# A PSUM bank by name for each TensorE task, in place of three banks in strict turn

## What is computed

```
x = x + tanh(g_xattn) * attention(layernorm(x), context)
x = x + tanh(g_ffn) * ffn(layernorm(x))

attention(x, c): q = rms(x Wq'), k = rms(c Wk'), v = c Wv'     (rms over the 8 values of each head)
                 softmax(q k' / sqrt(8)) v
ffn(x):          down(silu(gate(x)) * up(x))                   gate, up: 256 -> 704, down: 704 -> 256
                 weights are integers (w - 128) * scale
```

## Time and profile before

| | us |
|---|---|
| median of 3 runs | 269.2 |
| lowest, highest | 265.5, 272.75 |
| the profiled execution | 267.05 |
| its span in the trace | 265.2 |

### The profile page before, as it was taken

How to read it: one execution, slowest core, us unless ns; L and a number is a source line. 1 busy time by engine, 2 the same in 40 slices (tenths; PEclk the granted TensorE clock), 3 DMA queues, 4 the chain that set the end, 5 groups by cost and what they waited for, 6 DMA issues and landing times.

```text
span 265.2 us, 7329 instructions
## 1 busy us (share of the span) xinstructions
PE 219.6 (83%) x2592; PEld 178.5 (67%) x2592; DVE 176.5 (67%) x583; ACT 177.8 (67%) x338; POOL 106.3 (40%) x145
## 2 busy tenths in 40 slices
PE   1663979659879999899989989998999697965864
PEld 1553758437657878688777868786878585855764
DVE  4487999934665776687658765876596674657162
ACT  3258585844867895789578867885897667534250
POOL 5012212021322463645464455446444735434451
PEclk9999597956988999999999999999999999996799
DMA  5897522233075022603160406050506070000001
GB/s 178 216 352 178 62 56 49 54 45 62 0 101 101 0 56 49 136 3 72 26 138 0 87 12 138 0 100 3 121 0 82 13 109 2 21 22 0 20 20 40
DMA packets 45127, 18.08 MB, mean 68 GB/s; under 512 B 36400, under 2 KB 44848, under 8 KB 45104
## 3 DMA queue, kind: packets, MB, share of 16 engines
q1 hardware_dynamic: 45104, 17.77, 31.6%
HBM read 7.28 MB, written 2.10 MB: 35 GB/s over the span
## 4 chain that ended last, share of the span: by engine, by line
DVE 30%; PE 29%; issue 15%; POOL 14%; ACT 7%; DMA 2%; SPq 1%; DVEq 1%; POOLq 0%; ACTq 0%
PE bank L1278 7%; PE bank L1363 5%; POOL qk_parts L422 4%; POOL qk_unit L462 4%; PE pv_ps L1242 4%; POOL h_lo L430 4%; PE bank L1388 3%; DVE sums L899 3%; DVE hidden L990 3%; PE score_ps L1223 2%; PE bank L1311 2%; DVE silu L975 2%; DMA w_raw<-L_xattn_Wv_dram 2%; POOL x_all L439 2%; PE bank L1265 2%
## 5 line engine op out<-in xcount | busy, mean ns | idle before, releaser
L526 ACT ACTIVATE probs<-score_ps 128x1024 f32<-128x1024 f32 x64 | 65.9, 1032 | 3.5 <-PE score_ps L1223 3.5
L1363 PE MATMUL bank<-x_hi,gu_hi 128*128 128x256 f32 (+1 forms) x192 | 51.0, 301 | 4.7 <-DVE hidden L990 2.0
L462 POOL TENSOR_TENSOR qk_unit<-qk_raw,root_y 128x512 f32<-128x512 f32 x16 | 17.4, 1085 | 85.4 <-DVE root_y L783 85.4
L1363 PE MATMUL bank<-x_lo,gu_hi 128*128 128x256 f32 (+1 forms) x192 | 48.4, 286 | 0.0
L1242 PE MATMUL pv_ps<-probs,v_blocks 128*32 128x128 f32 x1024 | 42.8, 286 | 6.2 <-issue 4.2
L430 POOL TENSOR_TENSOR h_lo<-hidden,h_hi 128x256 fp32r<-128x256 f32 (+1 forms) x48 | 35.3, 745 | 24.8 <-ACT h_hi L651 24.4
L1363 PEld LDWEIGHTS bank<-x_hi,gu_hi 128*128 128x128 f32 (+1 forms) x192 | 35.3, 184 | 9.5 <-DVE hidden L990 2.4
L1363 PEld LDWEIGHTS bank<-x_lo,gu_hi 128*128 128x128 f32 (+1 forms) x192 | 35.5, 185 | 0.0
L1242 PEld LDWEIGHTS pv_ps<-probs,v_blocks 128*32 128x32 f32 x1024 | 24.9, 112 | 15.5 <-issue 7.4
L640 ACT ACTIVATE tanh_g<-bank,half_gate 128x256 f32<-128x256 f32 (+1 forms) x48 | 22.8, 475 | 18.2 <-PE bank L1363 16.0
L1278 PE MATMUL bank<-w_hi,xc_hi 128*128 128x256 f32 x96 | 31.7, 330 | 2.4 <-DVE xc_lo L889 2.4
(11 more groups left out here) (108 smaller groups left out, 435.2 us busy)
## 6 DMA issues: line engine op xcount, KB each, us to landing
ctx_sb<-ctx_dram SPq DMA_DIRECT2D x16, 128.0 KB, 2.6
out_dram<-x_all SPq DMA_DIRECT2D x16, 128.0 KB, 1.8
x_all<-x_dram SPq DMA_DIRECT2D x1, 1536.0 KB, 10.5
dn_int<-L_ffn_wq_down_dram SPq DMA_DIRECT2D x1, 704.0 KB, 6.7
gu_int<-L_ffn_wq_gate_dram SPq DMA_DIRECT2D x1, 640.0 KB, 4.6
gu_int<-L_ffn_wq_up_dram SPq DMA_DIRECT2D x1, 640.0 KB, 5.7
x_all<-x_dram SPq DMA_DIRECT2D x1, 384.0 KB, 5.1
w_raw<-L_xattn_Wq_dram SPq DMA_DIRECT2D x1, 256.0 KB, 2.7
```

The lines of the kernel that those rows point to most:

```text
L462: nc.gpsimd.tensor_tensor(qk_unit[:], qk_raw[:], root_y[:, 0:2 * H].unsqueeze(2).to_broadcast([P, 2 * H, HD]), ALU.mult).then_inc(unit_rea ...
L526: nc.scalar.activation(probs[:, t % 2, :], score_ps[t % 2][:].rearrange("p h n -> p (h n)"), ACT.Exp, scale=float(HD) ** 0.5 / UNIT ** 2). ...
L1363: last = nc.tensor.matmul(bank[k][0:r, a * TOK:(a + 1) * TOK], w[:, j, a, c, 0:r], xx[:, c, :], start=(n == 1), stop=(n == (4 if wide_weig ...
```

## The change

The order of the tasks stays. Each has now a bank by name:

| bank | before, in order | after, in order |
|---|---|---|
| 0 | turn0, qk0, ffn4, out1, turn2, ffn0 | turn0, qk0, ffn4, out1, y1 |
| 1 | out0, ffn2, ffn5, v1, y0, ffn1 | v0, ffn2, ffn5, v1, turn2, ffn1 |
| 2 | v0, ffn3, turn1, qk1, y1 | out0, ffn3, turn1, qk1, y0, ffn0 |

```
-    TASKS = ["turn0", "out0", "v0", "qk0", "ffn2", "ffn3", "ffn4", "ffn5", "turn1",
-             "out1", "v1", "qk1", "turn2", "y0", "y1", "ffn0", "ffn1"]
+    BANK_OF = {"turn0": 0, "out0": 2, "v0": 1, "qk0": 0, "ffn2": 1, "ffn3": 2, "ffn4": 0, "ffn5": 1, "turn1": 2,
+               "out1": 0, "v1": 1, "qk1": 2, "turn2": 1, "y0": 2, "y1": 0, "ffn0": 2, "ffn1": 1}
+    TASKS = list(BANK_OF)
...
     def use(p, task):
 
-        pos = TASKS.index(task)
+        pos, in_bank = TASKS.index(task), BANK_OF[task]
         q = p if isinstance(p, int) else FIRST_STEADY
-        n = sum(exists(i, t) for i in range(FIRST, q + 1) for k, t in enumerate(TASKS)
-                if k % NBANK == pos % NBANK and (i < q or k <= pos))
-        each = len(TASKS[pos % NBANK::NBANK])
-        return pos % NBANK, n if isinstance(p, int) else n + each * (p - FIRST_STEADY)
+        n = sum(exists(i, other) for i in range(FIRST, q + 1) for k, other in enumerate(TASKS)
+                if BANK_OF[other] == in_bank and (i < q or k <= pos))
+        each = list(BANK_OF.values()).count(in_bank)
+        return in_bank, n if isinstance(p, int) else n + each * (p - FIRST_STEADY)
```

## The result

| | before | after |
|---|---|---|
| median us | 268.73 (265.5 to 272.75, 4 runs) | 259.12 (257.91 to 259.8, 4 runs) |
| profiled execution us | 267.05 | 259.8 |
| its span us | 265.2 | 256.9 |

The changed kernel is faster: the ratio is 0.968, with a 95% interval of 0.958 to 0.977. Medians in this document are of all executions, ratios of those that took at most 1.5% more than the fastest of their kernel, so a ratio can differ a little from the quotient of two medians. Lines of the changed kernel stand 3 higher than those of before: L1265 is L1268, L990 is L993 and so on.

The account below looks back on a forecast made before the run. TensorE, busy 83% of the span, was taken as the bound. Steady rounds 3.8 us plus tail 3.2 less 0.1 in round 0 gave 6.9 us off the 269.2 us median: 262.3 us, range 257.5 to 268.5.

Parts of the forecast that it names:

- The bound and the wait: Mid-run: TensorE is the bound; turn0 idles 1.17 us a round for its bank alone, behind VectorE's late `hidden`.
- Steady rounds: Rounds 3 to 6, turn0 to qk0: 0.95 us gained a round, 3.8 us in four (2.0 to 4.7).
- At qk0: Round 5: qk0 follows v0 by 0.71 us and, 0.05 after `xc_lo`, starts at 161.02, 0.04 late.
- Shorter waits: Tasks with less cover, thinnest y0 behind qk1's copy (0.12 us less 0.05 delay): cost 0, bound 0 to 0.1 a round.
- C: Rival, y0 in rounds 2 to 6: qk1's copy slips, y0 loses 1.6 us a round, 270.4 us; chance 0.08.
- Round 0: Preparation under ffn0's name waits for y0's subtraction instead of turn2's: -0.1 us, bounded by 0 and 0.63.
- Tail: Rounds 7 to 9: 1.89 us kept through round 8 plus 1.29 in round 9, 3.2 us gained (1.5 to 4.5).
- The last group: Round 9, y0 and y1: only four products remain behind GpSimd's last `h_lo`; 1.29 us gained (0.7 to 1.51).
- the clock: Round 8: shorter gaps might keep the granted clock up, some 2.8 us more; left out of the sum, put in the range.
- D: Rival, whole round: the wait only moves, VectorE's chain closes the round; no gain, 269.2 us; chance 0.10.
- B: Rival at qk0: late `xc_lo` halves the gain to 0.5 us a steady round, 265.7 us; chance 0.22.

Follow-up runs that it names:

- this part alone: Changed kernel with the new banks kept in rounds -1 to 6 and the old strict turn in rounds 7 to 9: 263.02 us against 267.33, ratio 0.984.
- late-copy kernel: Changed kernel with ScalarE's copy of qk1, which frees y0's bank, put behind the next exponential: 263.37 us against 267.49, ratio 0.982.
- exchanged kernel: Changed kernel with the banks of turn0 and out0 exchanged in every round: 265.69 us against 267.33, ratio 0.991.
- the better table: Changed kernel with other banks for turn2, y0, y1, ffn0 and ffn1 in round 8 alone: 254.45 us against 269.01, ratio 0.950.
- either order tried on VectorE: Kernel before, old banks, VectorE's three qk_double copies moved behind both `hidden` (260.93 us, ratio 0.971) or behind the next round's `xc_lo` (262.75 us, ratio 0.978).

## Why the prediction came out as it did

The forecast was 262.3 us from 269.2, a ratio of 0.974; measured were 259.12 us and 0.968. The mechanism was right, and 6.9 us was short of the gain by terms that the sum did not hold.

**The bound and the wait.** Right. TensorE is the bound, and the idle at turn0 was for the bank alone.

**Steady rounds.** 0.95 us a round was worked out, 0.90 on average measured between out0 and out0 (0.92 in round 5), 3.60 in all for 3.8, and 3.59 with this part alone. Two steps hold as worked out: out0 0.05 behind ffn0's drain, v0 0.16 behind ffn1's. At qk0 two small errors offset each other. It follows v0 by 0.81 us in the kernel before (161.26 and 162.07), not 0.71, for the first two products of v0 are 0.23 apart. And `xc_lo`, an operand, reaches it not after 0.05 but after 0.15: in round 5 it ends at 158.57, and qk0 starts at 158.72, 0.83 behind v0. So qk0 shows no wait, and its cover is used up.

**Shorter waits.** y0 starts 0.12 us behind the copy in both kernels. The bound of 0 to 0.1 was right for the change. But I took 0.05 for the delay, and in the late-copy kernel y0 followed that copy by 0.13 in rounds 2 to 5 and by 0.05 in round 6, so in rounds 2 to 5 there was no cover left. C's price of 1.6 us a round was too high: it added the copy's own 0.6, which stands ahead of y0 in any order, and the wait was 1.1.

**Round 0.** I took -0.1. TensorE's preparation under ffn0's name started at 50.78 against 50.51, and the flag came 0.06 us earlier where the lead in round 0 had been 0.31 at its first out1. So 0.25 was lost up to the flag. No run isolates it, and by out0 of round 2 the lead was 0.65 again, for a reason that the record does not show.

**Tail.** out0 of round 7 gained 0.76 for 0.85; with turn2 it was 1.58 for 1.50, at ffn2 of round 8 2.73 for 2.72. turn2 gave back 0.96, where 0.83 was worked out. The last group gained 1.28 for 1.29. y0 of round 8 came 2.19 earlier for 1.89: turn2's part was 0.13 worse than worked out, and 0.42 was won between turn2 and y0, for turn2's transposes ran at full clock (0.68 us, before 1.11).

**What made it 8.3 in the trace and not 6.9.** Two things that the sum left out: the start (0.65, where the sum had -0.1) and the clock (1.0). The steady rounds (3.6 for 3.8) and the rest of the tail (3.1 for 3.2) were slightly less. The prediction named the clock as worth up to 2.8 us and could not place it; it had no term for the start. That both came out in favour is luck, as far as any run shows. These rows give the granted clock before and after around y0 and y1 of round 8. Before:

```profile
236.00:242.00 6.00, 3.17 (x25) 2.70 (x24) 5.08 (x17) 2.80 (x7) 2.50 (x4) 0.95 0.00 0
...
244.00:250.00 6.00, 6.00 (x30) 5.29 (x30) 0.69 (x1) 1.06 (x3) 2.43 (x4) 0.65 0.06 22
```

After:

```profile
236.00:238.00 2.00, 1.45 (x9) 1.46 (x10) 0.52 (x2) 1.09 (x3) 1.45 (x2) 0.76 0.00 0
...
238.00:242.00 4.00, 4.00 (x21) 3.29 (x20) 0.64 (x1) 0.37 (x1) 1.34 (x2) 0.69 0.00 0
```

With the earlier trace rows, TensorE spent (1 - 0.95) x 6 / 0.5 + 2 + (1 - 0.65) x 6 / 0.5 = 6.8 us at 1.2 GHz before, and (1 - 0.76) x 2 / 0.5 + (1 - 0.69) x 4 / 0.5 = 3.4 after. From y0 to ffn0 the lead grew by 0.62, and 0.42 came between turn2 and y0, 1.04 in all. Of the 6.8 us, 1.2 fell into the idle before turn2, which leaves 5.6 against 3.4; half of that difference is 1.1. The idle before turn2 was longer (3.75), and the stretch at half clock still shorter: the length of the last gap alone does not say what the clock does. The runs with other tables had 3.4, 6.8 or nothing here. That the clock fell less because of the edit is not shown.

**The measured 9.6 against 8.3.** The two profiled executions are 7.25 us apart, 1.05 less than their spans, since 1.85 us lie outside the span before and 2.9 after. The median of before lies 1.7 us above its profiled execution, that of the changed kernel 0.7 below its own: 7.25 + 1.7 + 0.7 = 9.6. The runs of before spread from 265.2 to 273.8 in the later sets of runs. My range took this spread as equal on both sides; the changed kernel spread over 1.9 us only. So 2.4 of the 9.6 us come from which executions were drawn, not from the edit as far as any run shows.

**The rivals.** D (no gain) and B (`xc_lo`) did not occur in the change, though qk0 had no cover left; B occurred, at 0.25 us a round, once VectorE's order was changed. C needs a slip that the order excludes. On the clock I had set the Trainium skill's rule ("TensorE: Matmul & The Clock Gate", section "A second HAM failure mode: psum-queue depth-cycling") aside, since the stretch of round 5 had 1.00 with that idle in it. That was too much to conclude from one execution. With an idle of the same 1.2 us the exchanged kernel fell to 1.2 GHz in three rounds of its profiled execution, and the kernel before did not in its own. The other statement, that double buffering in PSUM brought no further gain (the Trainium skill, "TensorE: Matmul & The Clock Gate", section "HAM oscillation — how this bites in real kernels"), is on another kernel and another edit, and says nothing about this one: who follows whom on a bank is worth 3.2% here, and 5.0% with the better table.

## What to carry to other kernels

A few buffers used in strict turn tie each task to whatever came so many places earlier. List for each task who had its buffer before and when that one is drained, and give early-drained buffers to the tasks that can start early; it costs no instruction. Look for it in the ramp and the last rounds too, where missing tasks change who follows whom: here they gave half of the gain, and a table of their own for one round gave another 4 us, of which about 1 was clock. Write down what cover is left at each claim, because a claim 0.12 us behind its drain makes a later harmless edit on another engine cost 4 us.

## What the runs showed of the hardware

- Where TensorE idled for a bank, it started 0.04 to 0.06 us after the end of the draining instruction at out0, out1, turn2, the ffn tasks and the last group. Before turn0 it was 0.12 to 0.15 in the rounds of the hardware loop (2 to 5) and 0.05 to 0.06 in round 6, in five kernels; before y0 in the late-copy kernel 0.13 in the four rounds of the loop and 0.05 in round 6. No run tells why these two tasks differ from the others in the loop. Where it idled for an operand (`xc_lo`, `x1n`, `x_lo`, `o_turned`) it was 0.14 to 0.15.
- The granted clock can fall in a full round: in the profiled execution of the exchanged kernel, the longest of ten, it was 0.52 for 3.5 us behind a stretch in which TensorE was busy 1.32 of 2.5 us, in three rounds one after the other, the first two of which took 27.3 and 27.2 us where those before them took 26.2 and 26.0. The kernel before had the same wait and the same busy share (1.33 of 2.5) in its profile and kept 1.00.
- TensorE's work alone gives a round of 24.65 us (25.83 less the wait, and 24.51 busy of 24.64 in a short round of one run), but with either order tried on VectorE the rounds settled at 24.9 to 25.1 us on average, and the new banks alone gave 24.9.
